# In the last round of an MLP loop, GpSimd's work goes to ScalarE and VectorE

## The chip, the cores and the metric

The kernel runs on one core of a Trainium2 chip. The metric is the device time of one execution in microseconds (us), lower is better. The core has five engines that work side by side and meet only at semaphores: TensorE (PE in the profile, matrix products), VectorE (DVE), ScalarE (ACT), GpSimd (POOL) and SyncE (SP), which here only issues DMAs.

## The reference

A small language-model tower over 8 sequences of 512 tokens with 128 channels, in float32:

```python
h = tok(x)                               # quantised embedding, 2-tap convolution, relu
h = h + attn(layernorm(h))               # a linear recurrence with a 64x64 matrix, 4 heads
h = h + ffn(layernorm(h))
def ffn(x):
    normed = (xf - mu) / sqrt(var + 1e-5) * ln_g + ln_b
    x_attn = normed @ attn_w.T + attn_b + xf
    tok = x_attn.reshape(2, 8, t, d)     # t = 256 tokens to an expert, fixed assignment
    h = gelu(tok @ fc1_w[e].T + fc1_b[e])            # 128 -> 512
    y = h @ fc2_w[e].T + fc2_b[e]                    # 512 -> 128
    return gelu(y @ next_w.T + next_b)
```

The change lies in `ffn` of the last sequence alone.

## The kernel before

First the embedding and the recurrence run (rounds j = -3 to -1 of the loop belong to them still), then the MLP in eight rounds j = 0 to 7, one sequence in each. Channels lie on the 128 partitions, tokens along the free dimension. A round has 8 units n = 0 to 7: half a sequence (256 tokens, `half = n // 4`, one expert to each half) by a quarter of the 512 hidden channels (`c = n % 4`). A unit is also called by its part number 8*j + n, so the last round holds the parts 56 to 63.

A part takes these steps. All matrix products of the MLP are made in a faster number format (float32r) and regain their precision by splitting both operands in a high part and a low part (the rounding error of the high part); three products of the parts are summed (L1072 and L1092, three 256-column matmuls each, `PARTS`).

1. TensorE, `fc1_part`: three matmuls into bank 5 (even n) or 6 (odd n), L1072.
2. ScalarE: gelu with the bias, from the bank to `hid_f` in float32 (L583). `hid_f` has four slots, so part m overwrites what part m-4 left there.
3. The high part: `hid_p[0]`. Up to round 5 ScalarE makes it by a second gelu from the same bank (L585). In rounds 6 and 7 (`j >= DVE_ROUND`) VectorE makes it by a copy that rounds, from `hid_f` (L736).
4. The low part: `hid_p[1] = hid_f - hid_p[0]`. Up to round 5 all are GpSimd's (L420); in rounds 6 and 7 GpSimd has the even n, VectorE the odd n (L740).
5. TensorE, `out_part`: three matmuls, L1092. The first two read the high part, the third the low part. Parts of one half add up in one bank.

When both halves of a sequence are summed, ScalarE takes the last gelu (`gelu_out`, L543, two instructions of 256 columns), an add with the transposed `h` gives `res` (GpSimd L442, in one instruction of 512 columns; for the last sequence VectorE L846, in two halves), and SyncE sends it to memory (L360, for the last sequence two DMAs at L365).

Nothing is scheduled at run time: each engine runs its instructions in the order in which the loops write them, and waits at semaphores. In round j TensorE runs `fc1_part(j, n)` and four parts behind it `out_part(8*j + n - 4)`; at n = 3 the out part comes before the fc1 part, because it completes the sequence before. The last four out parts (60 to 63) follow the loop. ScalarE puts `gelu_out(j - 1)` ahead of n = 3. GpSimd puts the add of `res` for sequence j-1 behind n = 5, and so in round 7 between the low parts of 60 and 62. `fc1_part` of part m waits until ScalarE has emptied the bank, that is for part m-2.

Of the kernel before, what the change touches and what calls it, by code (L numbers as in the profile page):

```python
# [36 lines left out]
ALU = mybir.AluOpType  # L37
# [56 lines left out]
def build(nc, ids, emb, conv, pack_a, pack_b, pack_c, fc1, fc2, out):  # L94
    with ExitStack() as ctx:
# [124 lines left out]
            sem("h_t_done"), sem("hT_ready"), sem("attn_done"), sem("xa_ready"))  # L220
        xa_t_done, xaT_ready = sem("xa_t_done"), sem("xaT_ready")
        fc1_done, hid_ready, o_done, gel_ready = sem("fc1_done"), sem("hid_ready"), sem("o_done"), sem("gel_ready")
        hid_lo_dve = sem("hid_lo_dve")
        fc1_split, fused_lo_ready, xaT_lo_ready, hid_lo_ready = (
            sem("fc1_split"), sem("fused_lo_ready"), sem("xaT_lo_ready"), sem("hid_lo_ready"))
        res_ready, last_res_ready = sem("res_ready"), sem("last_res_ready")
# [101 lines left out]
        def out_bank(b, half):  # L328
# [4 lines left out]
                return bank[half]  # L333
            return bank[0 if b == NB - 3 else 7]

        def wait_low(engine, part):

            k = part - 8 * DVE_ROUND
            if k < 0:
                engine.wait_ge(hid_lo_ready, part + 1)  # L340
            elif k % 2 == 0:
                engine.wait_ge(hid_lo_ready, 8 * DVE_ROUND + k // 2 + 1)
            else:
                engine.wait_ge(hid_lo_dve, k // 2 + 1)

        with nc.Block() as block:

            @block.sync
            def _(sp):
                sp.dma_start(emb_w[:], emb).then_inc(ld_emb, 16)  # L350
                sp.dma_start(ids_i[:], ids).then_inc(ld_ids, 16)
                sp.dma_start(pa[:], pack_a).then_inc(ld_pa, 16)
                sp.dma_start(pw[:, 1, :], pack_a[:, PA["a"]]).then_inc(ld_pa, 16)
                sp.dma_start(pb[:], pack_b).then_inc(ld_pb, 16)
                sp.dma_start(fc2_w[:].rearrange("p (e m) -> p e m", e=NE), fc2).then_inc(ld_fc2, 16)
                sp.dma_start(fc1_w[:], fc1).then_inc(ld_fc1, 16)
                for b in range(NB - 1):

                    sp.wait_ge(res_ready, b + 1)
                    sp.dma_start(out[b], res[:, b % 2, :]).then_inc(stored[b % 2], 16)  # L360
                for half in range(2):

                    b, s = NB - 1, slice(half * HALF, (half + 1) * HALF)
                    sp.wait_ge(last_res_ready, half + 1)
                    sp.dma_start(out[b][:, s], res[:, b % 2, s]).then_inc(stored[b % 2], 16)  # L365
                sp.wait_ge(stored[0], 16 * (NB // 2))
                sp.wait_ge(stored[1], 16 * (NB // 2 + 1))

            @block.gpsimd
            def _(pool):  # L370
# [40 lines left out]

                for j in range(-3, NB):
                    for n in range(8):
                        if 0 <= j < DVE_ROUND or (j >= DVE_ROUND and n % 2 == 0):

                            m, (half, c) = 8 * j + n, divmod(n, HC)
                            pool.wait_ge(hid_ready, m + 1)
                            if j >= 1:
                                pool.wait_ge(o_done, 2 * (j - 1) + half + 1)
                            nc.gpsimd.tensor_tensor(hid_p[1][:, half, c, :], hid_f[:, m % HID_SLOTS, :],  # L420
                                                    hid_p[0][:, half, c, :].bitcast(F32),
                                                    ALU.subtract).then_inc(hid_lo_ready, 1)
                        if j < 0:
                            for what, i in scan_work(j, n):
# [4 lines left out]
                                if what == "second":  # L429
# [1 line left out]
                                    pool.wait_ge(corr_ready, i + 1)  # L431
                                    nc.gpsimd.tensor_tensor(x_step(1, i), x_step(1, i), corr[:, i % CORR_SLOTS],
                                                            ALU.add).then_inc(x2_ready[1], 1)
                        if n == 5 and j >= 1:

                            o = j - 1
                            pool.wait_ge(gel_ready, o + 1)
                            pool.wait_ge(hT_ready, o + 1)
                            if o >= 2:
                                pool.wait_ge(stored[o % 2], 16 * (o // 2))  # L440
                            view = "p (s i k) -> p s i k"
                            nc.gpsimd.tensor_tensor(  # L442
                                res[:, o % 2, :].rearrange(view, s=2, i=T), gel[:, o % 2, :].rearrange(view, s=2, i=T),
                                hT[:, o % HT_SLOTS, :].rearrange("p (i s k) -> p s i k", s=2, i=T),
                                ALU.add).then_inc(res_ready, 1)
# [17 lines left out]
            def _(act):  # L463
# [84 lines left out]
                for j in range(-3, NB):  # L548
                    for n in range(8):
# [22 lines left out]
                        if j >= 0:  # L572
                            m, (half, c) = 8 * j + n, divmod(n, HC)
                            act.wait_ge(fc1_done, m + 1)
                            if m >= HID_SLOTS:
                                wait_low(act, m - HID_SLOTS)
                            if j >= 1:
                                act.wait_ge(o_done, 2 * (j - 1) + half + 1)
                            e = expert(j, half)
                            bias = pa[:, PA["fc1_b"]][:, e * HC + c:e * HC + c + 1]  # L580
                            src = bank[5 + n % 2][:, 0:HALF]

                            full = nc.scalar.activation(hid_f[:, m % HID_SLOTS, :], src, ACT.Gelu, bias=bias)  # L583
                            if j < DVE_ROUND:
                                nc.scalar.activation(hid_p[0][:, half, c, :], src, ACT.Gelu,  # L585
                                                     bias=bias).then_inc(hid_ready, 1)
                            else:
                                full.then_inc(full_ready, 1)
                        b = j + 1
                        if n == 1 and 0 <= b < NB:  # L590
                            act.wait_ge(xa_t_done, b + 1)
# [15 lines left out]
            def _(dve):  # L607
# [121 lines left out]
                def high_parts(j, places):  # L729
                    if DVE_ROUND <= j < NB:  # L730
                        for n in places:
# [1 line left out]
                            m = 8 * j + n  # L733
                            dve.wait_ge(full_ready, m + 1 - 8 * DVE_ROUND)
                            dve.wait_ge(o_done, 2 * (j - 1) + half + 1)
                            nc.vector.tensor_copy(hid_p[0][:, half, c, :],  # L736
                                                  hid_f[:, m % HID_SLOTS, :]).then_inc(hid_ready, 1)
                            if n % 2 == 1:
                                dve.wait_ge(hid_ready, m + 1)
                                nc.vector.tensor_tensor(hid_p[1][:, half, c, :], hid_f[:, m % HID_SLOTS, :],  # L740
                                                        hid_p[0][:, half, c, :].bitcast(F32),
                                                        ALU.subtract).then_inc(hid_lo_dve, 1)

                for j in range(-3, NB + 1):
# [90 lines left out]
                    if j == NB:  # L835
# [6 lines left out]
                        for n, s in enumerate([slice(0, 1), slice(1, 2)]):  # L842
                            if n == 1:
# [4 lines left out]
                                gel[:, o % 2, :].rearrange(view, s=2, i=T)[:, s],  # L848
                                hT[:, o % HT_SLOTS, :].rearrange("p (i s k) -> p s i k", s=2, i=T)[:, s],
                                ALU.add).then_inc(last_res_ready, 1)  # L850
                    if j < 0:
                        scan_part(j, [6, 7])
                    high_parts(j, range(6, 8))
# [2 lines left out]
            def _(pe):  # L856
# [198 lines left out]
                def fc1_part(b, n):  # L1055
# [6 lines left out]
                            pe.wait_ge(corr_ready, T)  # L1062
                            pe.wait_ge(fused_lo_ready, NE)
                    before = 8 * b + n - 2
                    if before >= 8 * DVE_ROUND:
                        pe.wait_ge(full_ready, before + 1 - 8 * DVE_ROUND)
                    elif before >= 0:
                        pe.wait_ge(hid_ready, before + 1)
# [7 lines left out]
                def out_part(part):  # L1076
# [3 lines left out]
                    if n == 0:  # L1080
# [4 lines left out]
                            pe.wait_ge(gel_ready, b - 1)  # L1085
                        elif b >= 1:
                            pe.wait_ge(gel_ready, b)
                    pe.wait_ge(hid_ready, part + 1)
                    for k, (w, m) in enumerate(PARTS):
                        if m == 1:  # L1090
                            wait_low(pe, part)
# [94 lines left out]
```

## Time and profile before

| what | us |
|---|---|
| three timed runs | 189.43, 189.66 (median), 189.98 |
| the profiled execution, its own time | 189.79 |
| its span, first to last instruction | 188.0 |
| TensorE matmul busy | 168.9 (90%) |
| VectorE busy | 136.7 (73%) |
| GpSimd busy | 111.0 (59%) |
| ScalarE busy | 107.4 (57%) |

The time of the profiled execution is 1.79 us longer than its span, since it has a start and an end around the instructions. The share of busy time is a mean over stages with different limits. TensorE's granted clock stands at full speed in all 40 slices of the span. Where instructions of one engine follow each other without a wait, the next one starts a little before the end of the last one in the profile; so the distance of two starts (the step) is what a row of instructions costs, not the duration of each.

### The profile page before, as it was taken

Reading aid. Unit: us, or ns where it says so; the run is one execution under the profiler, and the core shown is the slowest. Engines: PE = TensorE matmul, PEld = TensorE weight load, DVE = VectorE, ACT = ScalarE, POOL = GpSimd, SP = SyncE. Lnnn points to the kernel's source line nnn. Section 1 sums busy time; section 2 is a strip of 40 time slices with the busy share of each in tenths; the row PEclk is TensorE's granted clock in tenths of the full one; section 3 lists DMA queues with packets and bytes.
Section 4 is the critical chain, followed back from the end, with each engine's and each line's share of the span. In section 5 each row is a group of like instructions: output and inputs, shape, how many; then the busy total and the mean of one; then the engine's idle time right before and its main releaser. Section 6 shows DMA issues by size and latency. Waiting matters only on the chain.

```text
span 188.0 us, 3890 instructions
## 1 busy us (share of the span) xinstructions
PE 168.9 (90%) x1327; PEld 153.9 (82%) x1327; DVE 136.7 (73%) x409; ACT 107.4 (57%) x285; POOL 111.0 (59%) x178
## 2 busy tenths in 40 slices
PE   0497899999999998899898899999999999988972
PEld 0196779999999997787687799999998999987961
DVE  1859975765534546658988999998888896647993
ACT  3027997645543235434455484967949596775661
POOL 3106764799800000324979596696978969697761
PEclk9999999999999999999999999999999999999999
DMA  5994000000000000000000000000010100101103
GB/s 144 335 432 171 5 0 5 2 0 0 3 0 0 3 0 0 2 3 0 0 0 3 0 2 0 3 24 33 0 59 0 59 0 20 39 3 58 56 0 112
DMA packets 2327, 7.42 MB, mean 39 GB/s; under 512 B 254, under 2 KB 892, under 8 KB 2052
## 3 DMA queue, kind: packets, MB, share of 16 engines
q1 hardware_dynamic: 2162, 7.05, 10.0%
q8 instruction: 10, 0.16, 0.4%
q10 hardware_dynamic: 146, 0.13, 0.3%
q14 instruction: 9, 0.07, 0.1%
HBM read 5.09 MB, written 2.10 MB: 38 GB/s over the span
## 4 chain that ended last, share of the span: by engine, by line
PE 63%; POOL 10%; DVE 8%; ACT 8%; issue 7%; DMA 2%; POOLq 1%; ACTq 0%; DVEq 0%
PE bank L1072 8%; PE bank L934 8%; PE bank L1021 7%; PE bank L937 7%; PE bank L1092 6%; PE bank L962 5%; PE bank L1018 4%; PE bank L911 3%; PE bank L1041 3%; POOL hid_p L420 3%; PE bank L867 2%; PE bank L888 2%; ACT gel L543 2%; PE bank L951 2%; ACT hid_p L585 2%
## 5 line engine op out<-in xcount | busy, mean ns | idle before, releaser
L420 POOL TENSOR_TENSOR hid_p<-hid_f,hid_p 128x256 fp32r<-128x256 f32 x56 | 40.5, 745 | 16.7 <-ACT hid_p L585 12.5
L583 ACT ACTIVATE hid_f<-bank,pa 128x256 f32<-128x256 f32 x64 | 30.8, 485 | 13.4 <-PE bank L1072 12.7
L1072 PE MATMUL bank<-xaT_p,fc_p 128*128 128x256 f32 x192 | 35.0, 294 | 1.9 <-ACT corr L560 0.7
L1092 PE MATMUL bank<-hid_p,out_hi 128*128 128x256 f32 x128 | 32.2, 287 | 1.4 <-DVE hid_p L736 0.8
L492 ACT ACTIVATE X<-bank 128x128 f32<-128x128 f32 x64 | 17.6, 278 | 22.7 <-PE bank L937 22.5
L1072 PEld LDWEIGHTS bank<-xaT_p,fc_p 128*128 128x128 f32 x192 | 26.5, 189 | 4.7 <-issue 1.9
L1092 PEld LDWEIGHTS bank<-hid_p,out_hi 128*128 128x128 f32 x128 | 23.3, 188 | 2.5 <-POOL hid_p L420 1.4
L934 PE MATMUL bank<-uT,pa 128*128 128x128 f32 x128 | 25.2, 281 | 0.1
L585 ACT ACTIVATE hid_p<-bank,pa 128x256 fp32r<-128x256 f32 x48 | 23.5, 490 | 0.0
L937 PE MATMUL bank<-X,pa 128*128 128x128 f32 x120 | 23.2, 275 | 0.0
L427 POOL TENSOR_TENSOR E<-E,corr 128x248 f32<-128x248 f32 (+4 forms) x5 | 3.1, 625 | 32.0 <-ACT corr L568 32.0
L934 PEld LDWEIGHTS bank<-uT,pa 128*128 128x128 f32 x128 | 20.1, 191 | 1.5 <-ACT X L492 0.4
L1021 PE MATMUL bank<-pb,xh 128*128 128x128 f32 x128 | 19.5, 275 | 0.0
L937 PEld LDWEIGHTS bank<-X,pa 128*128 128x128 f32 x120 | 18.2, 192 | 0.0
L1092 PE MATMUL bank<-hid_p,out_lo 128*128 128x256 f32 x64 | 17.8, 278 | 0.0
L1021 PEld LDWEIGHTS bank<-pb,xh 128*128 128x128 f32 x128 | 16.9, 192 | 0.0
L962 PE MATMUL bank<-E,pw 128*128 128x256 f32 x60 | 16.2, 388 | 0.6 <-ACT corr L560 0.6
L657 DVE BATCH_NORM_STATS2 st<-h 128x6 f32<-128x128 f32 x64 | 13.9, 279 | 3.7 <-ACT h L504 3.4
L450 POOL TENSOR_TENSOR rstd<-spread,neg_half 128x8 f32<-128x8 f32 x8 | 13.2, 1649 | 1.3 <-DVE spread L806 1.3
L754 DVE SCALAR_TENSOR_TENSOR bank<-h,ratio,bank 128x128 f32<-128x128 f32 x32 | 9.0, 350 | 5.6 <-issue 5.6
L962 PEld LDWEIGHTS bank<-E,pw 128*128 128x128 f32 x60 | 10.1, 190 | 3.2 <-ACT corr L560 2.2
L1018 PE MATMUL bank<-pb,uT 128*128 128x128 f32 x64 | 12.3, 275 | 0.0
(124 smaller groups left out, 369.9 us busy)
## 6 DMA issues: line engine op xcount, KB each, us to landing
fc_w<-in_fc SPq DMA_DIRECT2D x2, 2048.0 KB, 12.5
out<-res SPq DMA_DIRECT2D x7, 256.0 KB, 2.0
pb<-in_pack_b SPq DMA_DIRECT2D x1, 320.0 KB, 3.7
pa<-in_pack_a SPq DMA_DIRECT2D x1, 279.0 KB, 3.0
out<-res SPq DMA_DIRECT2D x2, 128.0 KB, 1.7
pc<-in_pack_c ACTq DMA_DIRECT2D x1, 128.5 KB, 2.9
pw<-in_pack_a SPq DMA_DIRECT2D x1, 64.0 KB, 3.4
emb_w<-in_emb SPq DMA_DIRECT2D x1, 62.5 KB
```

Of the source, the lines that this page charges most:

```text
L420: nc.gpsimd.tensor_tensor(hid_p[1][:, half, c, :], hid_f[:, m % HID_SLOTS, :], hid_p[0][:, half, c, :].bitcast(F32), ALU.subtract).then_in ...
L492: nc.scalar.activation(X[:, g, s, i, :], src, ACT.Copy).then_inc(x_ready[g], 1)
L583: full = nc.scalar.activation(hid_f[:, m % HID_SLOTS, :], src, ACT.Gelu, bias=bias)
L585: nc.scalar.activation(hid_p[0][:, half, c, :], src, ACT.Gelu, bias=bias).then_inc(hid_ready, 1)
L657: last = nc.vector.bn_stats(st[:, b % 2, q, :], h[:, b, q * CH:(q + 1) * CH])
L934: last = mm(bank[6 + a][:, 0:w], pa[:, PA["b"]][:, a * P:(a + 1) * P], uT[:, g * GB:(g + 1) * GB, i, :], start=True, stop=(i == 0))
L937: last = mm(bank[6 + a][:, 0:w], a1, X[:, g, a * GB:(a + 1) * GB, i - 1, :], start=False, stop=True)
L962: mm(second_bank(g, i), a1 if i == 0 else pw[:, i + 1, :], E[:, g, :, :].rearrange("p a k -> p (a k)"), start=True, stop=True).then_inc(p2 ...
L1018: mm(dst, uT[:, b, q * TQ:(q + 1) * TQ, :].rearrange("p i k -> p (i k)"), pb[:, PB["d"]], start=True, stop=False)
L1021: last = mm(dst, xh[:, b % 2, a, q * P:(q + 1) * P], pb[:, PB["c"]][:, a * CH:(a + 1) * CH], start=False, stop=(a == NP - 1))
L1072: last = mm(bank[5 + n % 2][:, 0:HALF], fc1_p[w][:, e * HID + c * P:e * HID + (c + 1) * P], xaT_p[m][:, b % 2, half, :], start=(k == 0), s ...
L1092: last = mm(out_bank(b, half)[:, half * HALF:(half + 1) * HALF], out_p[w][:, e, c * CH:(c + 1) * CH], hid_p[m][:, half, c, :], start=(c == ...
```

## The change

In round 7 (`part >= LAST`, LAST = 56) GpSimd has no work left. For the even parts 56, 58, 60 and 62 ScalarE makes the high part by a second gelu from the bank, with a semaphore of its own (`last_hi_act`). VectorE drops the four rounding copies for them, and makes the low parts of all eight parts instead of four. The add of `res` for sequence 6, the last but one, goes from GpSimd to VectorE, behind the low part of part 61, in one instruction of 512 columns with a semaphore of its own (`late_res_ready`), for which SyncE's DMA now waits. Waits of TensorE, ScalarE and VectorE are turned to the new semaphores (`wait_high`, `wait_low`).

```diff
+        LAST = 8 * (NB - 1)
+        def wait_high(engine, part):
+            k = part - LAST
+            if k < 0:
+                engine.wait_ge(hid_ready, part + 1)
+            elif k % 2 == 0:
+                engine.wait_ge(last_hi_act, k // 2 + 1)
+            else:
+                engine.wait_ge(hid_ready, LAST + k // 2 + 1)
 ...
+            elif part >= LAST:
+                engine.wait_ge(hid_lo_dve, (LAST - 8 * DVE_ROUND) // 2 + part - LAST + 1)
 ...
-                        if 0 <= j < DVE_ROUND or (j >= DVE_ROUND and n % 2 == 0):
+                        if 0 <= j < DVE_ROUND or (DVE_ROUND <= j < NB - 1 and n % 2 == 0):
 ...
-                        if n == 5 and j >= 1:
+                        if n == 5 and 1 <= j < NB - 1:
 ...
+                            if j == NB - 1 and n % 2 == 0:
+                                nc.scalar.activation(hid_p[0][:, half, c, :], src, ACT.Gelu,
+                                                     bias=bias).then_inc(last_hi_act, 1)
 ...
-                            nc.vector.tensor_copy(hid_p[0][:, half, c, :],
-                                                  hid_f[:, m % HID_SLOTS, :]).then_inc(hid_ready, 1)
-                            if n % 2 == 1:
-                                dve.wait_ge(hid_ready, m + 1)
+                            if j < NB - 1 or n % 2 == 1:
+                                nc.vector.tensor_copy(hid_p[0][:, half, c, :],
+                                                      hid_f[:, m % HID_SLOTS, :]).then_inc(hid_ready, 1)
+                            if j == NB - 1 or n % 2 == 1:
+                                wait_high(dve, m)
 ...
+                    if j == NB - 1:
+                        o = j - 1
+                        dve.wait_ge(gel_ready, o + 1)
+                        dve.wait_ge(hT_ready, o + 1)
+                        dve.wait_ge(stored[o % 2], 16 * (o // 2))
+                        view = "p (s i k) -> p s i k"
+                        nc.vector.tensor_tensor(
+                            res[:, o % 2, :].rearrange(view, s=2, i=T), gel[:, o % 2, :].rearrange(view, s=2, i=T),
+                            hT[:, o % HT_SLOTS, :].rearrange("p (i s k) -> p s i k", s=2, i=T),
+                            ALU.add).then_inc(late_res_ready, 1)
 ...
-                    if before >= 8 * DVE_ROUND:
+                    if before >= LAST and n % 2 == 0:
+                        wait_high(pe, before)
+                    elif before >= 8 * DVE_ROUND:
                         pe.wait_ge(full_ready, before + 1 - 8 * DVE_ROUND)
```

VectorE, from part 60 to the end of the program. Before (the casts write high parts, the adds into `hid_p1` low parts):

```order
L736 CAST hid_p0<-hid_f 128x256 [waits o_done,full_ready] x2
L740 TENSOR_TENSOR hid_p1<-hid_f,hid_p0 128x256 [waits hid_ready]
L736 CAST hid_p0<-hid_f 128x256 [waits o_done,full_ready] x2
L740 TENSOR_TENSOR hid_p1<-hid_f,hid_p0 128x256 [waits hid_ready]
L846 TENSOR_TENSOR res<-gel,hT 128x256 [waits stored1,hT_ready,gel_ready]
L846 TENSOR_TENSOR res<-gel,hT 128x256 [waits gel_ready]
```

The same place in the changed program, whose line numbers are higher:

```order
L761 TENSOR_TENSOR hid_p1<-hid_f,hid_p0 128x256 [waits last_hi_act,o_done,full_ready]
L757 CAST hid_p0<-hid_f 128x256 [waits o_done,full_ready]
L761 TENSOR_TENSOR hid_p1<-hid_f,hid_p0 128x256 [waits hid_ready]
L879 TENSOR_TENSOR res<-gel,hT 128x512 [waits stored0,hT_ready,gel_ready]
L761 TENSOR_TENSOR hid_p1<-hid_f,hid_p0 128x256 [waits last_hi_act,o_done,full_ready]
L757 CAST hid_p0<-hid_f 128x256 [waits o_done,full_ready]
L761 TENSOR_TENSOR hid_p1<-hid_f,hid_p0 128x256 [waits hid_ready]
L867 TENSOR_TENSOR res<-gel,hT 128x256 [waits stored1,hT_ready,gel_ready]
L867 TENSOR_TENSOR res<-gel,hT 128x256 [waits gel_ready]
```

A cast and a low part in turn have become a low part, a cast and a low part for each pair, and the add for sequence 6 stands between the pairs 60/61 and 62/63.

ScalarE, the parts 56 to 60 (bank5 is an even part, bank6 an odd one; the two `gel` rows are sequence 6). Before:

```order
L583 ACTIVATE hid_f<-bank5,pa 128x256 [waits o_done,hid_lo_ready,fc1_done]
L583 ACTIVATE hid_f<-bank6,pa 128x256 [waits o_done,hid_lo_dve,fc1_done]
L583 ACTIVATE hid_f<-bank5,pa 128x256 [waits o_done,hid_lo_ready,fc1_done]
L543 ACTIVATE gel<-bank7,out_c 128x256 [waits res_ready,o_done]
L543 ACTIVATE gel<-bank7,out_c 128x256
L583 ACTIVATE hid_f<-bank6,pa 128x256 [waits o_done,hid_lo_dve,fc1_done]
L583 ACTIVATE hid_f<-bank5,pa 128x256 [waits o_done,hid_lo_ready,fc1_done]
```

And in the changed program:

```order
L600 ACTIVATE hid_f<-bank5,pa 128x256 [waits o_done,hid_lo_ready,fc1_done]
L607 ACTIVATE hid_p0<-bank5,pa 128x256
L600 ACTIVATE hid_f<-bank6,pa 128x256 [waits o_done,hid_lo_dve,fc1_done]
L600 ACTIVATE hid_f<-bank5,pa 128x256 [waits o_done,hid_lo_ready,fc1_done]
L607 ACTIVATE hid_p0<-bank5,pa 128x256
L560 ACTIVATE gel<-bank7,out_c 128x256 [waits res_ready,o_done]
L560 ACTIVATE gel<-bank7,out_c 128x256
L600 ACTIVATE hid_f<-bank6,pa 128x256 [waits o_done,hid_lo_dve,fc1_done]
L600 ACTIVATE hid_f<-bank5,pa 128x256 [waits o_done,hid_lo_dve,fc1_done]
L607 ACTIVATE hid_p0<-bank5,pa 128x256
```

Each even part has got a second instruction directly behind its first, ahead of the next part and of the two `gel` instructions. The orders of TensorE's matmuls and of SyncE's DMAs are unchanged.

## Rows read from the trace of the kernel before

**Rows 1.** Chain that ended last, from 176 us: start, length, what.
```profile
...
181.62 1.46 POOL res L442
...
184.09 0.75 PE bank L1092 x4
...
184.87 0.48 ACT gel L543
...
185.37 0.42 DVE res L846
```

**Rows 2.** Stretches: length, then busy PE, PEld, DVE, ACT, POOL, clock, DMA.
```profile
...
176.10:182.60 6.50, 6.10 (x48) 5.50 (x47) 6.08 (x14) 4.50 (x11) 3.91 (x6) 1.00 0.11 40
182.60:186.00 3.40, 1.24 (x6) 0.83 (x6) 2.44 (x5) 0.47 (x1) 1.21 (x2) 1.00 0.32 116
...
```

**Rows 3.** GpSimd in order of time: start, length, instruction, idle before and its releaser.
```profile
...
178.00 0.74 POOL L420 TENSOR_TENSOR hid_p<-hid_f,hid_p 128x256 fp32r<-128x256 f32 x1 [0.56 <-DVE hid_p L736]
...
181.62 1.46 POOL L442 TENSOR_TENSOR res<-gel,hT 128x512 f32<-128x512 f32 x1
183.31 0.73 POOL L420 TENSOR_TENSOR hid_p<-hid_f,hid_p 128x256 fp32r<-128x256 f32 x1 [0.23 <-DVE hid_p L736]
```

**Rows 4.** VectorE in order of time, last round.
```profile
...
177.64 0.48 DVE L736 CAST hid_p<-hid_f 128x256 fp32r<-128x256 f32 x2
178.16 0.86 DVE L740 TENSOR_TENSOR hid_p<-hid_f,hid_p 128x256 fp32r<-128x256 f32 x1
...
180.22 0.42 DVE L740 TENSOR_TENSOR hid_p<-hid_f,hid_p 128x256 fp32r<-128x256 f32 x1
180.56 0.49 DVE L736 CAST hid_p<-hid_f 128x256 fp32r<-128x256 f32 x2
181.08 0.86 DVE L740 TENSOR_TENSOR hid_p<-hid_f,hid_p 128x256 fp32r<-128x256 f32 x1
181.87 1.56 DVE L736 CAST hid_p<-hid_f 128x256 fp32r<-128x256 f32 x2
...
```

**Rows 5.** VectorE in order of time, an add of 512 columns in an earlier round.
```profile
...
161.25 0.68 DVE L797 TENSOR_TENSOR h<-h,bank 128x512 f32<-128x512 f32 x1
...
```

**Rows 6.** ScalarE in order of time, last round.
```profile
175.78 0.48 ACT L583 ACTIVATE hid_f<-bank,pa 128x256 f32<-128x256 f32 x1 [0.20 <-PE bank L1072]
...
177.52 0.47 ACT L583 ACTIVATE hid_f<-bank,pa 128x256 f32<-128x256 f32 x1 [0.55 <-POOL hid_p L420]
...
179.00 0.84 ACT L583 ACTIVATE hid_f<-bank,pa 128x256 f32<-128x256 f32 x2
180.19 0.47 ACT L583 ACTIVATE hid_f<-bank,pa 128x256 f32<-128x256 f32 x1 [0.35 <-PE bank L1072]
180.87 0.47 ACT L583 ACTIVATE hid_f<-bank,pa 128x256 f32<-128x256 f32 x1 [0.20 <-PE bank L1072]
181.55 0.47 ACT L583 ACTIVATE hid_f<-bank,pa 128x256 f32<-128x256 f32 x1 [0.21 <-PE bank L1072]
...
```

**Rows 7.** TensorE's matmuls in order of time, last round.
```profile
...
176.70 0.51 PE L1072 MATMUL bank<-xaT_p,fc_p 128*128 128x256 f32 x3
...
178.07 0.85 PE L1072 MATMUL bank<-xaT_p,fc_p 128*128 128x256 f32 x6
...
179.53 0.62 PE L1072 MATMUL bank<-xaT_p,fc_p 128*128 128x256 f32 x3 [0.27 <-ACT hid_f L583]
...
182.26 0.28 PE L1092 MATMUL bank<-hid_p,out_hi 128*128 128x256 f32 x1
183.29 0.39 PE L1092 MATMUL bank<-hid_p,out_hi 128*128 128x256 f32 x1 [0.75 <-DVE hid_p L736]
...
184.09 0.50 PE L1092 MATMUL bank<-hid_p,out_hi 128*128 128x256 f32 x2 [0.30 <-POOL hid_p L420]
...
```

**Rows 8.** SyncE's DMA issues in order of time, the last two.
```profile
...
184.68 1.48 SPq L365 DMA_DIRECT2D out<-res  x2
```

More of the change, by code:

```diff
@@ L222, in build @@
         fc1_done, hid_ready, o_done, gel_ready = sem("fc1_done"), sem("hid_ready"), sem("o_done"), sem("gel_ready")
-        hid_lo_dve = sem("hid_lo_dve")
+        hid_lo_dve, last_hi_act, late_res_ready = sem("hid_lo_dve"), sem("last_hi_act"), sem("late_res_ready")
         fc1_split, fused_lo_ready, xaT_lo_ready, hid_lo_ready = (
@@ L357, in _ @@
                 for b in range(NB - 1):
-                    sp.wait_ge(res_ready, b + 1)
+                    if b < NB - 2:
+                        sp.wait_ge(res_ready, b + 1)
+                    else:
+                        sp.wait_ge(late_res_ready, 1)
                     sp.dma_start(out[b], res[:, b % 2, :]).then_inc(stored[b % 2], 16)
@@ L1087, in out_part @@
                             pe.wait_ge(gel_ready, b)
-                    pe.wait_ge(hid_ready, part + 1)
+                    wait_high(pe, part)
                     for k, (w, m) in enumerate(PARTS):
```

## The prediction

> **What bounds the kernel now.** I read the chain that ended last first. From 176 us on it hardly names TensorE: its links are GpSimd's, above all the add of `res` for sequence 6, 181.62 to 183.08, then the last matmuls, ending at 184.84, one gelu of 0.48 and one add of 0.42 [rows 1]. The stretches say the same by engine. From 176.10 to 182.60 TensorE is busy for 6.10 of 6.50 us; from 182.60 to 186.00 it is busy for 1.24 of 3.40 [rows 2]. So round 7 is TensorE's up to 182.5 and somebody else's behind that.
>
> Who it is, stands in the order of time. TensorE finishes the out part of 61 with the matmul that starts at 182.26; then part 62's first matmul comes only at 183.29, after 0.75 of idleness that ends with VectorE's cast, and its third, at 184.09, after 0.30 that ends with GpSimd's low part [rows 7]. VectorE shows two casts that start at 181.87 and take 1.56 together, where such a pair takes 0.48 or 0.49 elsewhere [rows 4]. Just then GpSimd is in its add, 181.62 to 183.08 [rows 3]. And a low part on VectorE takes 0.86 where a low part of GpSimd began before it (178.16 against 178.00), and 0.42 at 180.22, where none runs [rows 3, 4]. The two engines keep each other waiting. ScalarE, meanwhile, sits idle for 0.20 to 0.55 before most of its gelus [rows 6].
>
> **The change, part by part.** Parts are named by number, "high" and "low" are their two halves. Steps, from start to start: two gelus that take 0.84 together and 0.48 each are 0.36 apart [rows 6]; two casts 0.20 (0.48 less 0.28); a low part without GpSimd 0.34 (180.22 to 180.56); from the start of a cast to its own low part 0.32 (second cast at 180.76, low part at 181.08) [rows 4]; six matmuls take 0.85 and one 0.28, so a matmul's step is 0.11 and a part's 0.34 [rows 7].
>
> 1. *Second gelus on ScalarE, four.* The first gelu of 56 starts at 175.78, so its second runs from 176.14 to 176.61. TensorE's fc1 of 58, which now waits for it, started at 176.70 already [rows 6, 7]: 0.09 to spare. Gelu 58 at 177.52, its second 177.88 to 178.35; fc1 of 60 stands at 178.07 + 0.34 = 178.41: 0.06 to spare. Gelu 60 starts at 179.36 (the second of the pair from 179.00), its second ends at 180.19; fc1 of 61 starts at 179.53, its last matmul at 179.87 (0.62 less 0.28), and out 57 lies between, so fc1 of 62 comes at 179.87 + 0.11 + 0.34 = 180.32: 0.13 to spare. Gelu 62 at 180.87, its second 181.23 to 181.70, after which gelu 63 starts at 181.59 instead of 181.55. Two of the four fall into gaps with less than 0.1 us over. I take nothing for it but the 0.04 on gelu 63, which nobody waits for in the end; the bounds are 0 and 3 x 0.36 = 1.08 on TensorE (the first rival).
>
> 2. *VectorE.* It loses four casts (4 x 0.20) and gains four low parts (4 x 0.34) and the add. Replayed from 177.64, where it came free: low 56 at 177.64, cast 57 at 177.98, low 57 at 178.30, low 58 at 178.64, free at 178.98. It waits for gelu 59, which ends at 179.47: cast 59 at 179.50, low 59 at 179.82. Low 60 waits for the second gelu: 180.22. Cast 61 waits for gelu 61 (180.19 + 0.47 = 180.66): 180.70, low 61 at 181.02. The add at 181.36. Low 62 behind it, cast 63 0.34 later, low 63 another 0.32 later.
>
> 3. *The add of 512 columns on VectorE.* No row shows this one there. The nearest is the add of 512 columns at L797, 0.68, one operand of which lies in a bank [rows 5]; 0.42 for 256 columns [rows 1] gives the same, with 0.26 for 256 more. Step: 0.68 less the usual overlap of 0.08 is 0.60. Bounds: 0.40 (two casts) and 1.38 (GpSimd's 1.46 less 0.08) [rows 3]. I take 0.60: low 62 at 181.96 to 182.38, cast 63 182.30 to 182.58, low 63 182.62 to 183.04.
>
> 4. *TensorE.* Behind 182.26 the slots run on by 0.11: part 62 from 182.37, its third matmul at 182.60, which has low 62 since 182.38. Part 63 from 182.71 (cast 63 ended 182.58), its third in the slot 182.94. Low 63 ends at 183.04, so that one waits, starts at 183.09 and takes 0.39 as the first after a wait does [rows 7]: end at 183.48. Without the wait it would be 182.94 + 0.28 = 183.22.
>
> 5. *GpSimd* loses four low parts and the add; what it still has, the low parts and the add of round 6, is unchanged, and with it the wait of gelu 58 for GpSimd (0.55 [rows 6]) stays.
>
> 6. *The tail* from the last matmul to the end, 188.0 - 184.84 = 3.16, stays: gelu, add, DMA [rows 1, 8]. The first half's add on VectorE starts at 182.96, behind low 63, and is out of the way when the second is due at 184.02. SyncE's DMA for sequence 6 goes out a microsecond earlier, and those of sequence 7 start at 183.4 and 184.5 instead of 184.68 and about 185.8 [rows 8].
>
> Sum: 184.84 - 183.48 = 1.36 off the span, 188.0 to 186.64. With the 1.79 around the span that is 188.43 for the profiled execution, which ran 0.13 above the median of the timed runs (189.79 against 189.66); so I forecast 189.66 - 1.36 = 188.3. If no wait were left at all it would be 188.0 (gain 1.62); if the add cost as on GpSimd, the end would come 0.78 later, 189.1.
>
> **The rivals.**
>
> *ScalarE's second gelus reach TensorE.* The spare times 0.09, 0.06 and 0.13 are small beside the 0.05 that a release takes here (low 62 ends at 183.31 + 0.73 = 184.04, TensorE starts at 184.09 [rows 3, 7]). TensorE is full from 178 to 182.5 but for one gap of 0.27 before fc1 of 61, and what it loses it doesn't get back. If each of fc1 58, 60 and 62 slips by a whole gelu, 1.08 is lost and the gain is 0.28: 189.4. For it speaks that the slack is below what I can read off; against it, that a slip is likelier some hundredths than 0.36, since ScalarE starts each pair at the time it started before.
>
> *VectorE becomes the bound, and the kernel slower.* Place: the eight low parts and the add. Price: suppose 0.86 is what a low part costs on VectorE when it follows a cast, whatever GpSimd does; most of them in this round do take that. Then the step is 0.78, the add doubles to 1.36 with a step of 1.28, and the replay goes: low 59 at 180.62, low 60 at 181.40, low 61 at 182.50, the add at 183.28, low 62 at 184.56, low 63 from 185.66 to 186.52, last matmul to 186.96: 2.12 later than now, 191.8. It decides from a low part of about 0.63 on: behind gelu 59 five low parts and the add, which counts twice, lie in a row, seven times the excess, and 7 x 0.2 eats up 1.36. Against it stands the row at 180.22: 0.42, behind a cast, with GpSimd idle [rows 4].
>
> [...]
>
> *The gain is there, but something else ends last*: the add of sequence 6, now ahead of low 62, delays low 62 and low 63, or the tail stretches because the last three DMAs follow each other more closely. The first is in the sum (0.26 between 183.48 and 183.22); the second has a room of about 1 us between issues, as before. I give it 0.3 us at most: 188.6.
>
> **How the numbers follow.** Forecast with its small slips (187.9 to 188.9): 0.83. ScalarE reaches TensorE in earnest: 0.09, of which a quarter still ends faster. VectorE bound, slower: 0.04. Something that no row shows, to either side: 0.04. A measurement of this kernel can tell some 0.3% (0.57 us) from no change; faster therefore means below 189.1, slower above 190.2. Faster: 0.83 + 0.02 + 0.01 = 0.86; same 0.09; slower 0.05. The forecast's own range runs from no wait left, 188.0, less 0.1 for the spread of the runs, to three slips of 0.1 with the add at the price of two halves (0.14 more) and 0.2 of spread. The range of 8 in 10, 187.8 to 189.0, adds a little on both sides, above for the nearer cases of the first rival.
>
> **What would show it.** Right: in the changed trace TensorE has no wait over 0.2 us between 179.6 and the last matmul, which ends at about 183.5; VectorE's low parts from 56 on take 0.42 each; its add of 512 columns takes about 0.68; the four second gelus take 0.47 and nobody's idle time is put down to them; the chain ends low part, matmul, gelu, add. Wrong: idle time of TensorE before fc1 58, 60 or 62 released by ScalarE (first rival), low parts of 0.6 and more with GpSimd silent (second), or a last matmul at 183.5 with a span above 187.

## The result, and the profile after

The changed kernel takes 188.18 us (median of 6 runs, 188.00 to 188.72) against 189.56 for the kernel before on the same chip (189.41 to 189.98): ratio 0.9926, 95% interval 0.9914 to 0.9938. Forecast were 188.3 and a gain of 1.36; measured are 188.18 and 1.38. Two repetitions, further down, put the gain at 1.0 and 1.6 by their ratios.

The profiled execution, at 188.72 with a span of 186.9, was the slowest of the six. Its first gelu of the MLP, far ahead of everything that was changed, starts at 102.4, where the kernel before has 102.2, and gelu 56 starts at 176.13 instead of 175.78. So I don't compare clock times between traces but the time from the start of gelu 56, the first of the last round, to the end of the last matmul: 184.83 - 175.78 = 9.05 before, 183.75 - 176.13 = 7.62 after, 1.43 less. From there to the end of the span it is 3.17 in both.

The chain that ended last, from 176 us on (start, length, what), to be set beside [rows 1]:

```profile
177.66 0.13 issue
177.79 0.07 ACT hid_f L600
177.86 0.30 issue
178.17 0.41 ACT hid_p L607
...
178.92 0.46 ACT gel L560
179.38 0.38 ACT hid_f L600
...
181.83 1.93 PE bank L1126 x15
183.77 0.02 issue
183.79 0.48 ACT gel L560
184.27 0.02 issue
184.30 0.42 DVE res L867
```

GpSimd has gone from it. Now it is TensorE's, with a piece of ScalarE's at 177.8 to 179.8: gelu 58 and its second gelu, the gelu of sequence 6, gelu 59. The stretches say where the time was (same columns as [rows 2]):

```profile
176.10:182.60 6.50, 6.37 (x51) 5.96 (x51) 5.85 (x16) 5.75 (x15) 1.05 (x2) 1.00 0.11 40
182.60:186.00 3.40, 1.15 (x9) 0.81 (x7) 1.44 (x5) 0.62 (x2) 0.00 (x0) 0.95 0.43 153
```

Up to 182.60 TensorE does 51 matmuls instead of 48. ScalarE's 5.75 us instead of 4.50 are the four second gelus, and VectorE is less busy than before (5.85 against 6.08) although it has more to do. VectorE in order of time, against [rows 4]:

```profile
180.10 0.93 DVE L761 TENSOR_TENSOR hid_p<-hid_f,hid_p 128x256 fp32r<-128x256 f32 x2
180.96 0.29 DVE L757 CAST hid_p<-hid_f 128x256 fp32r<-128x256 f32 x1
181.29 0.43 DVE L761 TENSOR_TENSOR hid_p<-hid_f,hid_p 128x256 fp32r<-128x256 f32 x1
181.63 0.68 DVE L879 TENSOR_TENSOR res<-gel,hT 128x512 f32<-128x512 f32 x1
182.23 0.42 DVE L761 TENSOR_TENSOR hid_p<-hid_f,hid_p 128x256 fp32r<-128x256 f32 x1
182.57 0.29 DVE L757 CAST hid_p<-hid_f 128x256 fp32r<-128x256 f32 x1
182.89 0.43 DVE L761 TENSOR_TENSOR hid_p<-hid_f,hid_p 128x256 fp32r<-128x256 f32 x1
```

Each low part takes 0.42 or 0.43; the 0.86 and the pair of casts of 1.56 are gone. The add of 512 columns takes 0.68, with a step of 0.60, as was taken for it. Low 63 ends at 183.32, and TensorE's last matmul waits for it:

```profile
178.34 0.97 PE L1106 MATMUL bank<-xaT_p,fc_p 128*128 128x256 f32 x6
...
183.14 0.28 PE L1126 MATMUL bank<-hid_p,out_lo 128*128 128x256 f32 x1
183.37 0.38 PE L1126 MATMUL bank<-hid_p,out_hi 128*128 128x256 f32 x1
```

Between the last two lies 0.23 instead of 0.11; in [rows 7] the waits in this place were 0.75 and 0.30. Note the first row too: six matmuls took 0.97, where they took 0.85 before. There, at fc1 of 60, TensorE has had to wait for a second gelu of ScalarE.

### The profile page after: what moved, and what is told of

It reads as the page before. It is cut to its first block, busy times and chain, and to the rows that moved or that the text cites. A ratio compares the mean times of both kernels' runs of the same rounds, so it can differ in the third digit from the quotient of the medians.

```text
span 186.9 us, 3886 instructions
## 1 busy us (share of the span) xinstructions
PE 169.2 (91%) x1327; PEld 154.3 (83%) x1327; DVE 135.4 (72%) x410; ACT 108.6 (58%) x289; POOL 106.5 (57%) x173
## 4 chain that ended last, share of the span: by engine, by line
PE 53%; POOL 14%; DVE 12%; issue 9%; ACT 8%; DMA 2%; ACTq 0%; POOLq 0%; DVEq 0%
PE bank L966 8%; PE bank L969 7%; PE bank L1106 6%; POOL hid_p L437 6%; PE bank L1126 5%; PE bank L994 5%; PE bank L1053 4%; POOL rstd L467 3%; PE bank L943 3%; PE bank L899 2%; PE bank L920 2%; PE bank L983 2%; PE bank L1050 2%; ACT gel L560 2%; POOL X L449 2%
## 5 line engine op out<-in xcount | busy, mean ns | idle before, releaser
L437 POOL TENSOR_TENSOR hid_p<-hid_f,hid_p 128x256 fp32r<-128x256 f32 x52 | 37.5, 741 | 14.5 <-ACT hid_p L602 12.6
```

## The experiments

The theory: VectorE and GpSimd shut each other out, as the pair of casts of 1.56 us beside GpSimd's add (0.48 or 0.49 elsewhere) and the low parts of 0.86 beside GpSimd's (0.42 elsewhere) made likely, and what is gained is the time that VectorE stood behind GpSimd's instructions and GpSimd behind VectorE's casts. The rivals: the gain is that of the second gelus, which save VectorE four casts; or that of the add alone; or the waits were a chain of semaphores, with no shared resource in it. All numbers together; "round" is the time from the start of gelu 56 to the end of the last matmul in the profiled execution, the ratio is to the kernel before on the same chip, with its 95% interval.

| kernel | us | ratio | round |
|---|---|---|---|
| before | 189.56 | 1 | 9.05 |
| changed | 188.18 | 0.9926 (0.9914, 0.9938) | 7.62 |
| changed, again (r1) | 188.65 | 0.9946 (0.9934, 0.9958) | 7.71 |
| changed, again (r3) | 188.09 | 0.9916 (0.9901, 0.9931) | 7.70 |
| e1: before, add on VectorE only | 189.35 | 0.9976 (0.9966, 0.9987) | 8.58 |
| e4: before, high parts on ScalarE only | 189.13 | 0.9966 (0.9955, 0.9977) | 8.46 |
| e2: changed, add back on GpSimd | 188.34 | 0.9932 (0.9917, 0.9947) | 7.71 |
| e5: changed, idle add on GpSimd | 189.53 | 0.9987 (0.9976, 0.9998) | 8.78 |
| e6: changed, idle memsets on GpSimd | 188.50 | 0.9932 (0.9913, 0.9950) | 7.77 |
| e7: changed, all high parts on ScalarE | 188.77 | 0.9953 (0.9939, 0.9966) | 8.17 |
| e3: changed, add behind low 59 | 187.97 | 0.9910 (0.9893, 0.9926) | 7.65 |
| r2: the same as e3 | 188.47 | 0.9937 (0.9924, 0.9951) | 7.62 |
| e8: changed, gelu of sequence 6 behind gelu 63 | 188.24 | 0.9923 (0.9909, 0.9937) | 7.35 |
| e9: changed, the same behind gelu 61 | 188.25 | 0.9925 (0.9905, 0.9946) | 7.60 |

e1 to e4 ran on one chip, r1, r2, e5 and e7 on a second, r3, e6 and e8 on a third, e9 on a fourth. The changed kernel itself comes out at 0.9926, 0.9946 and 0.9916 in three comparisons. The last two differ by 0.3%, and their intervals don't overlap. So 0.3% between comparisons on different chips means nothing; r1 was expected at 0.9926 and r3 at 0.9926 to 0.9946, and neither came there. The small effects below rest on the traces, one for each run; in the three of the changed kernel the round is 7.62 to 7.71.

**One part of the change alone (e1, e4).** e1 is the kernel before with the add moved:

```diff
-                        if n == 5 and j >= 1:                       # GpSimd
+                        if n == 5 and 1 <= j < NB - 1:
 ...
+                    if j == NB - 1:                                 # VectorE, behind low 61
+                        nc.vector.tensor_tensor(res[:, o % 2, :]..., ALU.add).then_inc(late_res_ready, 1)
```

> The kernel before with one part of the change: the add of res for sequence 6 goes from GpSimd to VectorE, behind low 61; high parts and low parts stay as before. Theory (VectorE and GpSimd shut each other out, and GpSimd's add of 1.46 us was the largest piece of it): the pair of casts 62/63 is no longer held up, but low 62 stays on GpSimd behind cast 62 and holds up low 63 on VectorE; replayed, the last matmul ends about 0.5 us earlier than before, about 189.0. Rival A (the gain comes from the second gelus on ScalarE, which spare VectorE its casts): no gain, 189.6. Rival B (the add alone was the trouble): the whole gain, 188.2.

Measured: 189.35, 0.45 less than before by the ratio, and the round is 0.47 shorter. That is the theory's 0.5; both rivals are out. VectorE in e1, in order of time:

```profile
182.03 0.68 DVE L861 TENSOR_TENSOR res<-gel,hT 128x512 f32<-128x512 f32 x1
182.63 0.48 DVE L739 CAST hid_p<-hid_f 128x256 fp32r<-128x256 f32 x2
183.15 0.85 DVE L743 TENSOR_TENSOR hid_p<-hid_f,hid_p 128x256 fp32r<-128x256 f32 x1
```

GpSimd in the same kernel:

```profile
182.99 0.73 POOL L423 TENSOR_TENSOR hid_p<-hid_f,hid_p 128x256 fp32r<-128x256 f32 x1 [1.17 <-DVE hid_p L739]
```

The casts 62 and 63 take their 0.48 again. But GpSimd's low 62 starts only at 182.99, behind cast 62, and low 63 on VectorE stands beside it for 0.85.

e4 is the kernel before with the second gelus; GpSimd keeps its low parts and the add, and waits for ScalarE:

```diff
+                            if j == NB - 1 and n % 2 == 0:          # ScalarE
+                                nc.scalar.activation(hid_p[0][:, half, c, :], src, ACT.Gelu, bias=bias).then_inc(last_hi_act, 1)
 ...
-                            pool.wait_ge(hid_ready, m + 1)
+                            wait_high(pool, m)
 ...
-                            nc.vector.tensor_copy(...)               # VectorE: all parts
+                            if j < NB - 1 or n % 2 == 1:
+                                nc.vector.tensor_copy(...)
```

> The kernel before with one part of the change: the high parts of 56, 58, 60 and 62 come from a second gelu on ScalarE, and VectorE's four casts for them are gone; GpSimd keeps its four low parts and the add. Theory: GpSimd's low parts start earlier, since they no longer wait for VectorE's cast, and the add moves forward by some 0.65 us, but it still shuts VectorE out, now at low 61 and cast 63: last matmul about 0.6 us earlier than before, 188.9 to 189.1. Rival A (the second gelus are the gain): 188.2. Rival B (only taking work off GpSimd helps): 189.6.

Measured: 189.13, the round 0.59 shorter. GpSimd's add comes 5.19 behind gelu 56 instead of 5.84 and now shuts out low 61 and, with low 62, cast 63. VectorE in e4:

```profile
180.72 1.40 DVE L756 TENSOR_TENSOR hid_p<-hid_f,hid_p 128x256 fp32r<-128x256 f32 x1
182.05 0.82 DVE L752 CAST hid_p<-hid_f 128x256 fp32r<-128x256 f32 x1
182.90 0.42 DVE L756 TENSOR_TENSOR hid_p<-hid_f,hid_p 128x256 fp32r<-128x256 f32 x1
```

GpSimd in e4:

```profile
180.50 1.34 POOL L454 TENSOR_TENSOR res<-gel,hT 128x512 f32<-128x512 f32 x1
181.80 0.91 POOL L432 TENSOR_TENSOR hid_p<-hid_f,hid_p 128x256 fp32r<-128x256 f32 x1
```

Each part alone brings a third to a half of the change (0.45 and 0.65 by the ratios, of 1.40; 0.47 and 0.59 of 1.35 to 1.43 by the rounds). That the rest comes from the low parts leaving GpSimd is argued only, since no run has the two parts together with GpSimd's low parts kept.

**Where GpSimd's add costs (e2).** The changed kernel with the add on GpSimd again (the condition `n == 5 and j >= 1` restored, VectorE's add taken out).

> The changed kernel with the add of res for sequence 6 back on GpSimd, which has nothing else in the last round and so starts it as soon as gelu of sequence 6 is done, 2.5 us earlier than before the change. Theory: it holds up cast 59 by about 1.1 us, at a place where VectorE has some slack left; replayed, low 63 ends 0.09 later than in the changed kernel: 188.2 to 188.3. Rival (a GpSimd add beside VectorE costs its length wherever it stands): 0.8 to 1.1 us more, 189.0 to 189.3.

Measured: 188.34, the round 7.71: 0.09 longer than in the changed kernel's first trace, the figure expected, and no longer than in its two others. Cast 59 begins 0.32 inside GpSimd's add and ends 0.15 behind it, after 1.11 instead of 0.29. Counted from gelu 56, low 61 starts 0.61 later than in r3 (5.85 against 5.24). But VectorE has no add of its own to make behind it, a step of 0.60, and low 62 starts at 6.19 against 6.18. VectorE in e2:

```profile
179.27 1.11 DVE L754 CAST hid_p<-hid_f 128x256 fp32r<-128x256 f32 x1 [0.43 <-ACT hid_f L597]
180.42 0.76 DVE L758 TENSOR_TENSOR hid_p<-hid_f,hid_p 128x256 fp32r<-128x256 f32 x2
```

GpSimd in e2:

```profile
178.95 1.28 POOL L456 TENSOR_TENSOR res<-gel,hT 128x512 f32<-128x512 f32 x1 [1.73 <-ACT gel L557]
```

So the move of the add to VectorE, which by itself shortened the round of the kernel before by 0.47 (e1), is not needed once GpSimd has no low parts: in that case it can start 2.5 us earlier (3.38 behind gelu 56 instead of 5.84), where VectorE has room.

**Is it a shared resource? (e5, e6)** Both are the changed kernel with work on GpSimd that nobody waits for:

```diff
+                        if n == 5 and j == NB - 1:
+                            pool.wait_ge(hid_lo_dve, (LAST - 8 * DVE_ROUND) // 2 + 6)
+                            nc.gpsimd.tensor_tensor(spare[:, 0:L], h[:, 0, :], h[:, 1, :], ALU.add)   # e5
+                            nc.gpsimd.memset(spare[:, 0:L], 0.0)                                        # e6, instead of the add
+                            nc.gpsimd.memset(spare[:, L:2 * L], 0.0)
```

> The changed kernel with one instruction more: behind low 61 GpSimd adds two old tiles of h (512 columns) into unused memory; nobody waits for it. Theory (the two engines shut each other out while both have SBUF operands): it starts when VectorE's add of 512 columns is running or ends, holds the engine off for about 1.3, and low 62, cast 63 and low 63 come after it: last matmul 0.9 to 1.2 later, 189.1 to 189.4. Rival (what the change removed were waits along semaphores, GpSimd behind VectorE behind GpSimd, and no shared resource): no change, 188.2.

> The changed kernel with two memsets of 512 columns on GpSimd behind low 61 in place of the added add, into the same unused memory; they read nothing. [...] From gelu 56 to the last matmul 7.6 to 8.0 (7.7 in the changed kernel, 8.78 with the add), time within 0.3 of the changed kernel's. Rival (any GpSimd instruction on SBUF stops VectorE): as with the add, 0.9 to 1.1 later.

e5: 189.53, 0.88 slower than the changed kernel on the same chip, and the round 1.07 longer than its 7.71 (expected 0.9 to 1.2). No semaphore leads from this add to anything, so semaphores alone don't explain the waits, and the engines don't meet only at semaphores, as the description of the chip at the start has it. VectorE in e5:

```profile
181.11 0.69 DVE L882 TENSOR_TENSOR res<-gel,hT 128x512 f32<-128x512 f32 x1
181.71 1.51 DVE L764 TENSOR_TENSOR hid_p<-hid_f,hid_p 128x256 fp32r<-128x256 f32 x1
183.15 0.28 DVE L760 CAST hid_p<-hid_f 128x256 fp32r<-128x256 f32 x1
```

GpSimd in e5:

```profile
181.28 1.67 POOL L453 TENSOR_TENSOR spare<-h 128x512 f32<-128x512 f32 x1 [4.08 <-DVE hid_p L764]
```

VectorE's add, which began first, takes its 0.69; GpSimd's, begun inside it, takes 1.67 instead of 1.28 to 1.34; low 62, begun inside that, takes 1.51 instead of 0.42 and ends 0.28 behind it. In this trace the one that began later took longer, in both directions.

e6: 188.50, the round 7.77, against 188.09 and 7.70 of the changed kernel on the same chip. The round is within the 7.6 to 8.0 expected; the time is 0.41 longer, where at most 0.3 was expected, but the intervals of the ratios overlap. VectorE in e6:

```profile
180.84 0.69 DVE L883 TENSOR_TENSOR res<-gel,hT 128x512 f32<-128x512 f32 x1
181.45 0.42 DVE L765 TENSOR_TENSOR hid_p<-hid_f,hid_p 128x256 fp32r<-128x256 f32 x1
181.78 0.34 DVE L761 CAST hid_p<-hid_f 128x256 fp32r<-128x256 f32 x1
```

GpSimd in e6:

```profile
180.99 0.53 POOL L453 MEMSET spare<- 128x512 f32 x1 [4.07 <-DVE hid_p L765]
181.46 0.53 POOL L454 MEMSET spare<- 128x512 f32 x1
```

The add and the low part lie beside the memsets, the low part from end to end, and keep 0.69 and 0.42; only the cast, 0.34 instead of 0.28, ends later, 0.13 behind the second memset. So the two traces differ by what GpSimd ran: beside its add, which reads two tiles, a low part of VectorE took 1.51; beside its memsets, which read nothing, the add and a low part kept their length. The casts were held up by GpSimd's add in e2 (1.11 instead of 0.29) and a little by its memset in e6 (0.34 instead of 0.28). What it is that the two engines share, no run here shows.

How much of the gain is this blocking? No run separates it from another piece: GpSimd is the slower engine for this work (0.74 for a low part, VectorE 0.42), and its queue holds low 62 behind the add. An estimate from the rows of the kernel before, with nobody held up (GpSimd's add at 1.34, as for sequence 5 at 174.79, its low parts at 0.74, VectorE's casts at 0.28 and low parts at 0.42): the add runs from 181.2 to 182.55, low 62 to 183.25, the last matmul to 184.04 instead of 184.83. So about 0.8 of the 1.35 to 1.43 is the blocking, and about 0.55 is GpSimd's own queue, which the change takes away as well.

**ScalarE's side (e7).** All eight high parts by a second gelu, no cast on VectorE in the last round:

```diff
-                            if j == NB - 1 and n % 2 == 0:          # ScalarE, and the waits alike
+                            if j == NB - 1:
```

> The changed kernel with the high parts of all eight parts of the last round by a second gelu on ScalarE, and no cast on VectorE. It tests the rival that ScalarE's second gelus reach TensorE, by doubling them. Replayed: fc1 of 61 now waits for the second gelu of 59 and comes 0.35 later, fc1 of 63 some 0.05 for that of 61, while VectorE, without casts, is done earlier; last matmul 0.1 to 0.35 later than in the changed kernel, 188.3 to 188.5. If ScalarE had room enough: 188.0 to 188.2. If ScalarE were already at its limit with four: 1.4 later, 189.6.

Measured: 188.77 against 188.65 of the changed kernel on the same chip, 0.12 more, where 0.1 to 0.35 was replayed. The intervals overlap, so the times alone don't tell the two apart; but the round is 0.46 longer, more than the 0.35 replayed and five times the spread of the changed kernel's rounds. The place is the one named. TensorE in e7:

```profile
179.12 0.28 PE L1124 MATMUL bank<-hid_p,out_hi 128*128 128x256 f32 x1
179.90 0.63 PE L1104 MATMUL bank<-xaT_p,fc_p 128*128 128x256 f32 x3 [0.50 <-ACT hid_p L605]
```

fc1 of 61 stands 0.78 behind the matmul ahead of it, and waits for a second gelu. In the trace four second gelus fit but for some hundredths, eight do not.

**Looking for what is left (e3, r2, e8, e9).** The changed kernel's add stands behind low 61; e3 has it behind low 59:

```diff
                     high_parts(j, range(2, 4))
+                    if j == NB - 1:   # the add for sequence 6, taken from behind high_parts(j, range(4, 6))
```

> The changed kernel with VectorE's add of res for sequence 6 one place earlier, behind low 59 instead of low 61. Theory: VectorE has slack there; low 62 then waits for its second gelu only, low 63 ends before TensorE's slot for it and the last wait of TensorE (0.11 in the changed kernel's trace, and 0.11 of restart) is gone: last matmul 0.2 to 0.26 earlier, 187.9 to 188.0. Rival (the last wait hangs on ScalarE's second gelu of 62 or on gelu 63, not on VectorE's queue): no change, 188.2.

> The changed kernel with the add for sequence 6 behind low 59, once more, to set it against the changed kernel on one chip. In its first profile VectorE's low 63 was done before TensorE's slot, but TensorE's matmuls kept a step of 0.118 instead of 0.113 to the end, and the last one ended as late after gelu 56 as in the changed kernel (7.65 against 7.63). Theory (VectorE's queue is the last wait): 0.2 faster than the changed kernel in the same call, ratio 0.9910 to 0.9916. Rival (the longer step of the matmuls gives it back, whenever TensorE does not wait): the same as the changed kernel, 0.9924 to 0.9930.

> The changed kernel once more, unaltered, beside the next three on the same chip. Ratio to the kernel before 0.9926, as in the first comparison (188.2 where before is 189.6).

e3's 187.97 is the time expected, but the changed kernel didn't run on that chip. Beside it on one chip (r2) it is 188.47 against 188.65, ratios 0.9937 and 0.9946: not told apart, and outside both ranges that were expected of r2. The last wait did go: in e3's trace, as in r2's, the last matmuls follow without a gap. But the round stays at 7.65 and 7.62, because they follow more slowly. TensorE in e3:

```profile
182.41 0.40 PE L1126 MATMUL bank<-hid_p,out_hi 128*128 128x256 f32 x2
182.65 0.28 PE L1126 MATMUL bank<-hid_p,out_lo 128*128 128x256 f32 x1
182.76 0.40 PE L1126 MATMUL bank<-hid_p,out_hi 128*128 128x256 f32 x2
183.00 0.28 PE L1126 MATMUL bank<-hid_p,out_lo 128*128 128x256 f32 x1
183.12 0.34 PE L1126 MATMUL bank<-hid_p,out_hi 128*128 128x256 f32 x1
```

Three matmuls from 182.41 to 182.76 and from 182.76 to 183.12: 0.118 a step, where r3's trace has 0.113 (181.61 to 182.29, six steps). Over the 22 matmuls behind fc1 of 62 that is 0.1, and the last one, though low 63 is done 0.1 ahead of it, takes 0.34 instead of 0.28. That is most of the 0.2 to 0.26 looked for, and it is what r2's rival says.

e8 and e9 take up the wait of fc1 61 for gelu 59, which was in the kernel before already (0.27, [rows 7]): the gelu of sequence 6 stands ahead of gelu 59 on ScalarE, and nobody needs it soon.

```diff
-                        if n == LAG - 1 and j >= 1:
+                        if n == LAG - 1 and 1 <= j < NB - 1:              # e8, and gelu_out(NB - 2) behind the
+                                                                          # loop, the add behind low 63
+                        if n == (LAG - 1 if j < NB - 1 else 6) and j >= 1:   # e9, the add behind low 61
                             gelu_out(j - 1)
```

> The changed kernel with gelu of sequence 6 (two instructions) moved on ScalarE from ahead of gelu 59 to behind gelu 63, and the add for sequence 6 on VectorE behind low 63. Theory: the one wait of TensorE that is left in the last round (0.3 and a restart, fc1 of 61 for gelu 59) goes, since gelu 59 no longer stands behind the two; replayed, gelu 59 at 178.62 on the clock of the kernel before, gelu 61 at 179.75, gelu 63 at 181.19, last matmul to 182.81: 7.0 to 7.2 from gelu 56 to the last matmul instead of 7.63 to 7.71, 0.4 to 0.6 faster than the changed kernel, unless the tail grows, because the DMAs of sequence 6 and 7 now follow each other within 0.8. Rival (the parts go on as fast as ScalarE can make them, and the order of its instructions is indifferent): no change.

> The changed kernel, unaltered, as the reference for the next two on one chip: ratio to the kernel before 0.9926 to 0.9946, as in the two comparisons before.

> The changed kernel with gelu of sequence 6 on ScalarE behind gelu 61 instead of ahead of gelu 59; the add for sequence 6 stays on VectorE behind low 61. Theory, from the trace with that gelu behind 63 (7.35 from gelu 56 to the last matmul, but a tail 0.27 longer with three DMAs within 0.9): TensorE's wait for gelu 59 is gone here too, gelu 62 and 63 come 0.25 later than there, low 63 is done about 0.1 behind its slot: 7.4 to 7.55, and since the DMA of sequence 6 goes out more than a microsecond ahead of the next the tail is 3.17 again. 0.15 to 0.3 faster than the changed kernel: ratio 0.990 to 0.992 to the kernel before. Rival (what is won by the order of the gelus is lost again, here to gelu 62 and 63): 0.992 to 0.9945 and 7.6 to 7.7.

e8: the round is 7.35, 0.35 shorter than r3's 7.70 on the same chip, and the wait of fc1 61 for gelu 59 is gone but for 0.03. The 7.0 to 7.2 expected was missed all the same: fc1 of 62 now waits for the second gelu of 60, with its restart some 0.14, and behind it the matmuls keep the step of 0.118. Yet the time is 188.24 against 188.09: the tail grew from 3.17 to 3.44, and the rest is within the spread. The DMA issues of SyncE in e8:

```profile
182.81 0.33 SPq L377 DMA_DIRECT2D out<-res  x1
183.18 0.94 SPq L382 DMA_DIRECT2D out<-res  x2
```

And in r3:

```profile
182.08 0.33 SPq L377 DMA_DIRECT2D out<-res  x1
183.41 1.40 SPq L382 DMA_DIRECT2D out<-res  x2
```

In e8 all three go out within 1.3 us, in r3 within 2.7, and the last one lands 1.95 behind its issue instead of 1.73; with a little later issue 0.27 of the 0.35 goes there. e9 keeps the DMA of sequence 6 early and the tail at 3.16, which speaks for that cause. But its gelu of sequence 6 pushes gelu 62 and 63 back; low 62, cast 63 and low 63 then each come just behind their slot, and each costs TensorE a restart of about 0.1. The round is 7.60 and the ratio 0.9925, the rival's case. Neither beats the changed kernel.

## Why the prediction was right

Point by point, by its own steps. r3's trace serves best for it, since its gelu 56 starts at the same 175.78 as in the kernel before.

1. *What bounds the end.* VectorE and GpSimd keeping each other waiting was right, and e5 shows it without any semaphore between them. The forecast didn't need its share: the replay gives all the work to VectorE and ScalarE, and so takes away GpSimd's slow queue together with the blocking (about 0.55 and 0.8 by the estimate above). The rival with 0.86 as VectorE's own price fell: every low part of the last round from 56 on took 0.41 to 0.43.
2. *Second gelus on ScalarE.* Taken at nothing. The times were right (second gelu of 60 at 179.71, of 62 at 181.28, forecast 179.72 and 181.23). What was mis-sized is the room: fc1 of 58 and 60 had 0.09 and 0.06 over, but in these traces a release takes 0.05 (in the changed kernel's first trace low 63 ends at 183.32, the matmul starts at 183.37), and a matmul that has waited keeps the next one off for up to 0.22 instead of 0.11 (fc1 of 61 takes 0.62 for its three, where 0.50 is usual), or for 0.15 where it was a matter of hundredths (fc1 of 62 in r3, 0.54). So both slipped by 0.1. TensorE in r3:

```profile
178.07 0.96 PE L1106 MATMUL bank<-xaT_p,fc_p 128*128 128x256 f32 x6
...
179.53 0.62 PE L1106 MATMUL bank<-xaT_p,fc_p 128*128 128x256 f32 x3 [0.16 <-ACT hid_f L600]
...
183.10 0.38 PE L1126 MATMUL bank<-hid_p,out_hi 128*128 128x256 f32 x1
```

The six matmuls take 0.96 instead of 0.85. It cost nothing, because TensorE waits behind both places anyway: for GpSimd's low part of 54 at 177.50 (177.49 before), and for gelu 59 at 179.53, as before. Behind that, fc1 of 62 slipped by 0.04. The first rival was thus at work, for 0.04 in the end.
3. *VectorE's queue and the add.* Low 62 forecast at 181.96, measured 181.97 in r3; low 63 forecast 182.62 to 183.04, measured 182.62 to 183.05. The add took 0.68 with a step of 0.60. One term was off: low 60 was forecast at 180.22, 0.03 behind its second gelu, and came at 180.33. Cast 61 waits for gelu 61 anyway, so nothing came of it.
4. *TensorE's end.* Forecast 183.48, measured 183.10 + 0.38 = 183.48.
5. *Tail.* 3.16 forecast, 3.17 measured.

Two of the signs named didn't come as written. The chain ends matmul, gelu, add, with no low part before the matmul, though the last matmul waits for low 63; and it runs over a second gelu (`hid_p` L607, 0.41 at 178.17), where nobody was to wait for one. In the working of the range, the add in two halves is 0.08 dearer by its own steps (2 x 0.34 against 0.60), not 0.14; the range doesn't hang on it.

That it is exact to the hundredth is luck in part: the slip of 0.04 and the longer steps of some matmuls fell in where TensorE waited 0.11 for low 63 at the end, and the changed kernel's own first trace has 7.62 instead of 7.70. That the timed gain agrees within 0.02 is luck altogether: the same two kernels gave 1.0 and 1.6 in the other comparisons.

## What to carry to other kernels

Where instructions of one engine take longer beside those of another (low 62 took 1.51 instead of 0.42 in e5), read the long duration against what the other engine has begun just before, and ask also what the slower engine's queue would cost if nobody held it up. The cure here was to give the work of the last, unhidden stretch to engines whose instructions kept their length beside each other (ScalarE's second gelus 0.46 to 0.49, VectorE's low parts 0.41 to 0.43), or to place the intruding instruction where the other has slack (e2 gained as much as the full move). A replay of the queues, instruction by instruction with the steps of the rows, carried here to a hundredth of a microsecond for the change, to about a tenth for e1, e4, e2 and e7, and missed e8 by 0.15 or more; what it needs is the release time (here 0.05), the cost of a restart (here 0.04 to 0.11), and who absorbs a slip.

A wait that is taken away shows the next one, and it may lie outside the engines: e8 shortened the round by 0.35 and got a tail 0.27 longer, up to the landing of the last DMA.

## What was not expected of the hardware

- Matmuls of the same form, with the granted clock at 1.00 in both, mostly followed each other in these traces at one of two steps, 0.113 or 0.118, and kept it for up to twenty and more in a row: 0.113 in the kernel before from 179.99 to 182.3, 0.118 in e3, r2 and e8 over the same out parts. In the last round the step changed mostly at a wait or within some seven matmuls behind one, but in r3 also some twenty behind (the two steps from 182.63 to 182.87 take 0.24). What chooses it stays open; over the 55 matmuls from gelu 56 on it is worth up to 0.25.
- The same unchanged start of the program puts the first gelu of the MLP at 102.2 in the kernel before, 102.4 in the changed one and 101.6 in e4 and e8. That is as large as half of what was to be measured here, and a reason to compare stretches, not clock times. Its cause was not looked for.
